# The skewing copies of the distances issued by three queues, in a two-layer decoder kernel on one core

## The chip, the cores and the metric

The kernel is one program for one core of one Trainium2 chip. The metric is the device time of one execution in microseconds (us), the median of several runs. Engines: TensorE (PE in the profile), VectorE (DVE), ScalarE (ACT), GpSimd (POOL) and SyncE (SP). A DMA is issued by an instruction in the queue of SP, ACT or POOL.

## The reference, cut to what matters

Two decoder layers over x (8 batches of 112 tokens, width 256). Each adds, in turn, a self-attention, a part that looks at the context (8 x 375 x 256), and a mixture of experts. The change lies in the context part of the first layer, a dynamic time warping (DTW) of the 375 context rows against the 112 tokens, for each batch:

```python
D = _pairwise_euclidean(small, large)         # 375 x 112
R = _dtw_cost(D)    # r = d_ij + min(up, left, diag)
i_idx, j_idx, valid = _backtrack(R, T_small, T_large)
contrib = small[i_idx] * valid[:, None].astype(small.dtype)
expanded = jnp.zeros((T_large, d), dtype=small.dtype).at[j_idx].add(contrib)
```

and `x = x + _L0_xattn_ref(ctx_1024, _layernorm(x, axis=-1))`. Everything after it (the first layer's experts, the second layer) needs its result.

## The kernel before, in words

Each engine has its own function with its instructions in the order written there; semaphores tie them together (`wait_ge`, `then_inc`). A DMA adds 16 to its semaphore when it has landed.

**Distances.** `Dd` (in `Vc_r`) holds them with the 112 tokens on partitions and, for each of B = 8 batches, S = 375 values. They are made two batches at a time (`q4` = 0 to 3): VectorE's `squares`, four activations on ScalarE (L976 to L979), and VectorE's `roots` (L1731 to L1733), whose last instruction raises `dist_ready`.

**Skewing copies.** The recurrence runs on 32 partitions, G = 4 groups of context columns (RC = 94 values each, 93 in the last, g = 3) times 8 batches; partition g * 8 + b of `Dsk` holds group g of batch b, shifted by 4 steps per group. A DMA copy for each (b, g) and for each block of token rows brings them there: its source is one run of up to 94 values in each of the block's partitions, its destination one partition. The blocks k are the rows 0 to 15, 16 to 47 and 48 to 111 (`ROW_CUTS`), with 32 copies each. Before, SyncE issues the 24 copies of g = 0 to 2 of each block (L569 for block 0, L573 for blocks 1 and 2) and GpSimd the 8 of g = 3 (L742, L745). Both take block 0 pair by pair as `dist_ready` rises.

**Recurrence.** VectorE goes through 124 columns q, each with two scans over half a group (L1768) and the minima that feed them (L1763). Before columns 1, 17 and 49 it waits for all 32 copies of block 0, 1 and 2. SyncE brings the finished cost rows to another layout behind it (L581, 56 copies), and VectorE goes on with the choices and the path (L1798 and after).

**Beside it.** Behind the squares ScalarE empties TensorE's banks of the second layer's key products (12 copies into `KcT_r`); then it waits for all three blocks of copies, because the value products are written over `Dd` (12 copies into `Vc_r`). Behind its copies GpSimd sets an edge (L746), waits for the value products and reloads the context (L751), used after the path is known.

Of the kernel before, what the change touches and what calls it, by code (L numbers as in the profile page):

```python
# [57 lines left out]
def view(t, offset, dims, parts=None):  # L58

    x = t[:] if parts is None else t[parts[0]:parts[1]]  # L60
    return bass.AP(x.tensor, x.offset + offset, [x.ap[0]] + dims)
# [8 lines left out]
def decoder_kernel(nc, A, out):  # L70
    B, T, D = A["x"].shape
# [4 lines left out]
    HB = B // 2  # L76
    HT = HB * T
    E0, F0 = A["L0_ffn_b1"].shape
    M0 = F0 // 128
    E1, _, F1 = A["L1_ffn_Wg"].shape  # L80
    NS1 = A["L1_ffn_Sg"].shape[1] // F1
    WE = KD * 2 * F1 + D
# [4 lines left out]
    G = 4  # L87
# [13 lines left out]
    with ExitStack() as ctx:  # L101
# [3 lines left out]
        def sem(name):  # L105
            return ctx.enter_context(nc.semaphore(name))
# [245 lines left out]
        act, dve, routing, scored = "act", "dve", "routing", "scored"  # L352
# [69 lines left out]
        for n in range(NG + LV):  # L422
            if n < NG and n % 2 == 0:
                r_s1[n], r_s1[n + 1] = ring.take(scored, scored)
            if LT <= n < NG + LT:
                (r_pt1[n - LT],) = ring.take(act)
            if n >= LV:
                _, _, key, first, last = value_step(n - LV)
                if first:
                    r_o1[key] = ring.open(BANKS - 2 + key[1])  # L430
                if last:
                    ring.close(r_o1[key], act)
# [44 lines left out]
        ROW_CUTS = (0, 16, 48, T)  # L477
        NBLK = len(ROW_CUTS) - 1
# [19 lines left out]
        s = {name: sem(name) for name in names}  # L498
        ctx_loaded = [sem(f"ctx_loaded{i}") for i in range(4)]
        rows_moved = [sem(f"cost_rows_moved{k}") for k in range(NBLK)]  # L500
        last_rows_moved = [sem(f"last_cost_rows_moved{k}") for k in range(NBLK)]
        cw_moved = [sem(f"segment_rows_moved{i}") for i in range(SEG)]
        xg0_loaded = [sem(f"token_rows_loaded_first{i}") for i in range(XR)]
        y0_stored = [sem(f"tile_rows_scattered{i}") for i in range(YR)]
# [18 lines left out]
        def skewed(b, g, k):  # L523

            lo, hi = ROW_CUTS[k:k + 2]
            return view(Dsk, (g * KC + lo) * RC, [[RC, hi - lo], [1, min(RC, S - g * RC)]],
                        (g * B + b, g * B + b + 1))

        def plain_rows(b, g, k):

            src = Dd[ROW_CUTS[k]:ROW_CUTS[k + 1], b, g * RC:min((g + 1) * RC, S)]
            return bass.AP(src.tensor, src.offset, [src.ap[0], [1, min(RC, S - g * RC)]])


        def step_of(seg, g):
            return 2 * seg + 1 + g

# [2 lines left out]
        def column_done(q):  # L540


            return 4 * q + (q < COLS) + min(q - 1, COLS - SH - 1) // SH
# [8 lines left out]
        def _(sp):  # L552
# [9 lines left out]
                             c_d[:, 2 * i:2 * i + 2]).then_inc(ctx_loaded[i], 16)  # L562

            sp.wait_ge(s["dsk_clear"], 1)
            for q4 in range(B // 2):
                sp.wait_ge(s["dist_ready"], q4 + 1)
                for b in (2 * q4, 2 * q4 + 1):
                    for g in range(G - 1):
                        sp.dma_start(skewed(b, g, 0), plain_rows(b, g, 0)).then_inc(rows_moved[0], 16)  # L569
            for k in range(1, NBLK):  # L570
                for b in range(B):
                    for g in range(G - 1):
                        sp.dma_start(skewed(b, g, k), plain_rows(b, g, k)).then_inc(rows_moved[k], 16)  # L573

            sp.wait_ge(s["edge_ready"], 1)
            for seg in range(SEG):
                for g in range(G):
                    n = min(RC, S - g * RC)
                    sp.wait_ge(s["dtw_op"], column_done(KC * min(step_of(seg, g) + 1, STEPS)))
                    q = seg * SC + g * KC  # L580
                    sp.dma_start(Rb[seg * B:(seg + 1) * B, :, 1 + g * RC:1 + g * RC + n],  # L581
                                 RS[g * B:(g + 1) * B, q:q + SC + 1, 1:1 + n]).then_inc(s["costs_moved"], 16)
# [63 lines left out]
            for r in range(NS1):  # L646
                f = slice(r * F1, (r + 1) * F1)
# [20 lines left out]
        def _(pool):  # L668
# [67 lines left out]
            link(nc.gpsimd.memset(RS[:, 0:KC + 1, :], BIG))  # L736

            nc.gpsimd.memset(RS[0:B, 0, 0:1], 0.0).then_inc(s["costs_clear"], 1)
            for q4 in range(B // 2):
                pool.wait_ge(s["dist_ready"], q4 + 1)  # L740
                for b in (2 * q4, 2 * q4 + 1):
                    pool.dma_start(skewed(b, G - 1, 0), plain_rows(b, G - 1, 0)).then_inc(last_rows_moved[0], 16)  # L742
            for k in range(1, NBLK):
                for b in range(B):
                    pool.dma_start(skewed(b, G - 1, k), plain_rows(b, G - 1, k)).then_inc(last_rows_moved[k], 16)  # L745
            nc.gpsimd.memset(Rb[:, :, 0:1], BIG).then_inc(s["edge_ready"], 1)  # L746

            pool.wait_ge(full, r_vc[-1].n + 1)
# [41 lines left out]
            for n in range(NT0 + LAG):  # L790
# [6 lines left out]
                if 0 <= n - (LAG + 8) < 3 * KD:  # L797
                    k, w = divmod(n - (LAG + 8), 3)
# [83 lines left out]
        def _(sc):  # L882
# [90 lines left out]
            for q4 in range(B // 2):  # L973
# [4 lines left out]
                link(nc.scalar.activation(inv[:, sl, :], inv[:, sl, :], ACT.Exp, scale=-0.5))  # L978
                nc.scalar.activation(aaB[:, sl, :], inv[:, sl, :], ACT.Square).then_inc(s["inv_ready"], 1)  # L979

            sc.wait_ge(free[act], r_bias.count)
            i = 0
            for m in range(KD):
# [2 lines left out]
                         bias=bqk[:, 1, m:m + 1])  # L986
                    i += 1
            for k in range(NBLK):
                sc.wait_ge(rows_moved[k], 16 * B * (G - 1))
                sc.wait_ge(last_rows_moved[k], 16 * B)  # L990
            for i, slot in enumerate(r_vc):
                copy(slot, Vc_r[0:CR, 2 * i * D:(2 * i + 2) * D], bank(slot)[0:CR, :])
            for n, cols in enumerate((slice(NS // 2, NS), slice(0, NS // 2))):
# [69 lines left out]
            for n in range(NG + LV):  # L1063
                if n < NG:
                    sc.wait_ge(s["heads_shifted"], n + 1)
                    if n >= NP:
                        sc.wait_ge(full, r_pt1[n - NP].n + 1)
                    for j in range(HB):
                        ins = nc.scalar.activation(  # L1069
                            Px[:, n % NP, j * T:(j + 1) * T], bank(r_s1[n])[0:T, j * T:(j + 1) * T], ACT.Exp,  # L1070
                            bias=hm[:, n % NP, 1, j:j + 1], scale=HD ** -0.5, accum_out=hm[:, n % NP, 2, j:j + 1])
                    ins.then_inc(free[scored], 1)
                if LT <= n < NG + LT:
                    m = n - LT
                    if m >= 3:
                        sc.wait_ge(s["values_used"], m - 2)
                    copy(r_pt1[m], PxT[:, m % 3], bank(r_pt1[m])[0:T, 0:HT])
                if n >= LV:
                    _, _, key, _, last = value_step(n - LV)
                    if last:  # L1080
                        copy(r_o1[key], NT[:, key[0], x_cols(key[1])], bank(r_o1[key])[:, 0:HT])
# [548 lines left out]
        def _(ve):  # L1630
# [73 lines left out]
            for i, slot in enumerate(r_pv0):  # L1704
                src = bank(slot)
                for j in range(2):
                    b = 2 * i + j
# [47 lines left out]
            def step(ins):  # L1755
                ops[0] += 1
                ins.then_inc(s["dtw_op"], 1)
                return ops[0]

            def lesser(q, part, after):  # L1760
                lo, hi = part
                ve.wait_ge(s["dtw_op"], after)
                return step(v.tensor_tensor(mtmp[:, lo:hi], RS[:, q - 1, lo:hi], RS[:, q - 1, lo + 1:hi + 1], ALU.min))  # L1763

            def scan(q, part, after):
                lo, hi = part
                ve.wait_ge(s["dtw_op"], after)
                return step(v.tensor_tensor_scan(RS[:, q, lo + 1:hi + 1], mtmp[:, lo:hi],  # L1768
                                                 Dsk[:, (q - 1) * RC + lo:(q - 1) * RC + hi],
                                                 RS[:, q, lo:lo + 1], ALU.min, ALU.add))  # L1770
# [3 lines left out]
            lu = step(v.tensor_tensor(mtmp[:, 0:RC // 2], RS[:, 0, 0:RC // 2], RS[:, 0, 1:RC // 2 + 1], ALU.min))  # L1774
            for q in range(1, COLS + 1):
                if q - 1 in ROW_CUTS[:-1]:
                    ve.wait_ge(rows_moved[ROW_CUTS.index(q - 1)], 16 * B * (G - 1))
                    ve.wait_ge(last_rows_moved[ROW_CUTS.index(q - 1)], 16 * B)
                su = scan(q, upper, lu)
                ll = lesser(q, lower, sl) if q > 1 else \  # L1780
                    step(v.tensor_tensor(mtmp[:, RC // 2:RC], RS[:, 0, RC // 2:RC], RS[:, 0, RC // 2 + 1:RC + 1], ALU.min))
                if q < COLS:
                    lu = lesser(q + 1, upper, su)
                if q % SH == 1 and SH < q <= COLS - SH:

                    lu = step(v.stream_shuffle(RS[:, q + 1:q + 1 + SH, 0], RS[:, q - SH:q, RC],
                                               [(p - B) % 32 for p in range(32)]))
                sl = scan(q, lower, max(ll, su))
                assert sl == column_done(q)
# [334 lines left out]
            for n in range(B + 2):  # L2124
# [4 lines left out]
                if n >= 2:  # L2129
                    b = n - 2  # L2130
# [97 lines left out]
```

## Time and profile before

| | |
|---|---|
| median of 3 runs | 635.02 us (634.96 to 660.84) |
| the profiled execution's own time | 631.45 us |
| its span, first to last instruction | 629.5 us |
| mean granted TensorE clock | 0.888 of full speed |
| busy: PE / DVE / ACT / POOL | 472.0 / 400.3 / 234.3 / 185.8 us |
| DMA moved | 49.07 MB, mean 78 GB/s |

The span is what the profile covers; the execution's own time has 2 us around it. Issuing a DMA isn't counted as busy. Times inside the profile are us from the first instruction.

### The profile page before, as it was taken

What the parts mean: (1) busy time and instruction counts of PE and PEld (TensorE: products, weight loads), DVE (VectorE), ACT (ScalarE), POOL (GpSimd) and SP (SyncE); (2) the same over time, 40 slices, a digit from 0 to 9 for tenths busy, and PEclk for the clock granted to TensorE, in tenths of its full rate; (3) what the DMA queues carried; (4) which work ended last, traced back from release to release, by engine and by line L of the source; (5) the groups of instructions that cost most, each with busy time, mean ns of one, the idle gap of its engine ahead of it and who ended that gap; (6) DMA issues with size and microseconds to landing.
All of it is one profiled execution on the core that took longest, in us unless ns stands there. A gap on an engine that the chain in (4) does not pass through costs nothing.

```text
span 629.5 us, 9016 instructions
## 1 busy us (share of the span) xinstructions
PE 472.0 (75%) x2802; PEld 376.3 (60%) x2802; DVE 400.3 (64%) x1352; ACT 234.3 (37%) x670; POOL 185.8 (30%) x272
## 2 busy tenths in 40 slices
PE   6988999050002288699999996899999798799980
PEld 6974547040001035598899995778777475689850
DVE  6047765999989986453543257677874155756545
ACT  2357760030000421304344303389984545034300
POOL 6003260030000002135668324511102411366354
PEclk9988999675556599869999999999999999899995
DMA  5300111139410088712212140050005401045623
GB/s 169 116 24 1 37 28 24 37 55 149 72 16 0 10 269 274 163 26 68 69 55 72 50 134 1 2 169 1 2 2 156 145 1 59 27 135 167 136 85 115
DMA packets 48801, 49.07 MB, mean 78 GB/s; under 512 B 14656, under 2 KB 41908, under 8 KB 48532
## 3 DMA queue, kind: packets, MB, share of 16 engines
q1 hardware_dynamic: 40996, 33.37, 18.8%
q0 software_dynamic: 7760, 15.14, 10.2%
q8 instruction: 23, 0.38, 0.2%
q14 instruction: 22, 0.18, 0.1%
HBM read 36.14 MB, written 9.31 MB: 72 GB/s over the span
## 4 chain that ended last, share of the span: by engine, by line
PE 51%; DVE 28%; ACT 5%; issue 4%; SPq 4%; DMA 4%; POOL 2%; another core or an unknown queue 1%; DVEq 0%; ACTq 0%; POOLq 0%
PE ps L1143 45%; DVE big L1768 7%; PE ps L1146 6%; DVE mtmp L1763 4%; SPq L573 2%; DVE big L2118 1%; DVE rk L2110 1%; DVE big L1809 1%; DVE big L1810 1%; ACT N_r L921 1%; DVE big L1843 1%; SPq L569 1%; ACT big L893 1%; DMA big<-scattered 1%; DMA big<-in_L_attn_wo 1%
## 5 line engine op out<-in xcount | busy, mean ns | idle before, releaser
L1143 PE MATMUL ps<-ident 128*128 128x128 f32 (+1 forms) x304 | 63.2, 372 | 78.9 <-DVE big L1801 60.0
L1143 PEld LDWEIGHTS ps<-ident 128*128 128x128 f32 x304 | 46.0, 233 | 86.5 <-DVE big L1801 60.4
L1143 PE MATMUL ps<-ctxT_r,big 128*128 128x128 f32 (+1 forms) x616 | 83.2, 285 | 2.5 <-issue 1.2
L1143 PEld LDWEIGHTS ps<-ctxT_r,big 128*128 128x128 f32 (+1 forms) x616 | 75.8, 191 | 7.0 <-issue 5.0
L1768 DVE TENSOR_TENSOR_SCAN big<-mtmp,big 32x47 f32<-32x47 f32 x248 | 62.6, 287 | 11.6 <-DMA big<-Vc_r 11.6
L1143 PE MATMUL ps<-big 112*128 112x112 f32 (+6 forms) x458 | 61.6, 312 | 3.7 <-issue 3.4
L893 ACT ACTIVATE big<-ps 112x448 f32<-112x448 f32 (+5 forms) x63 | 38.4, 640 | 53.6 <-PE ps L1146 34.4
L1143 PEld LDWEIGHTS ps<-big 112*128 112x128 f32 (+5 forms) x458 | 51.7, 186 | 7.9 <-issue 4.3
L893 ACT ACTIVATE ctxT_r<-ps 128x256 f32<-128x256 f32 (+3 forms) x74 | 30.9, 433 | 60.5 <-PE ps L1146 34.6
L1146 PE MATMUL ps<-ident,big 112*112 112x112 f32 (+5 forms) x289 | 40.5, 277 | 13.4 <-DVE big L2118 4.4
L1146 PEld LDWEIGHTS ps<-ident,big 112*112 112x112 f32 (+5 forms) x289 | 30.5, 144 | 27.7 <-DVE big L1843 10.2
L1069 ACT ACTIVATE big<-ps,rk 112x112 f32<-112x112 f32 x128 | 44.4, 388 | 5.8 <-DVE rk L2111 5.3
L1143 PE MATMUL ps<-big,ctxT_r 128*128 x168 | 39.6, 379 | 0.0
L700 POOL TENSOR_SCALAR veps<-mv 112x2 f32<-112x2 f32 x24 | 5.6, 233 | 110.5 <-DVE mv L1656 76.0
L1763 DVE TENSOR_TENSOR mtmp<-big 32x47 f32<-32x47 f32 x246 | 37.1, 183 | 0.0
L2053 DVE COPY big<-ps 128x256 f32<-128x256 f32 x21 | 8.9, 424 | 43.8 <-PE ps L1143 41.1
L1143 PE MATMUL ps<-N_r,ctxT_r 128*125 128x256 f32 x96 | 23.5, 409 | 16.9 <-ACT Vc_r L893 16.9
L1043 ACT ACTIVATE ctxT_r<-ps,big 128x128 f32<-128x128 f32 x84 | 24.0, 368 | 31.0 <-PE ps L1143 31.0
L866 POOL DMA_INDIRECT ctxT_r<-normed,source x29 | 29.3, 1009 | 19.3 <-issue 9.9
L1143 PEld LDWEIGHTS ps<-big,ctxT_r 128*128 128x128 f32 x168 | 30.4, 190 | 3.3
L1143 PEld LDWEIGHTS ps<-N_r,ctxT_r 128*125 128x125 f32 x96 | 19.6, 205 | 21.1 <-ACT Vc_r L893 17.4
L794 POOL DMA_INDIRECT ctxT_r<-normed,source x21 | 25.5, 1213 | 21.5 <-PE ps L1146 12.5
(269 smaller groups left out, 927.7 us busy)
## 6 DMA issues: line engine op xcount, KB each, us to landing
big<-in_L_ffn_W SPq DMA_DIRECT2D x16, 512.0 KB, 7.2
routed<-Vc_r SPq DMA_DIRECT2D x29, 128.0 KB
big<-in_ctx SPq DMA_DIRECT2D x4, 750.0 KB
ctxT_r<-in_ctx POOLq DMA_DIRECT2D x4, 750.0 KB, 20.5
big<-in_L_ffn_Wg SPq DMA_DIRECT2D x16, 128.0 KB, 2.4
big<-in_L_ffn_Wu SPq DMA_DIRECT2D x16, 128.0 KB, 2.5
big<-in_L_ffn_Wd SPq DMA_DIRECT2D x16, 128.0 KB, 2.5
normed<-N_r SPq DMA_DIRECT2D x2, 896.0 KB, 5.3
```

The lines of the kernel that those rows point to most:

```text
L569: sp.dma_start(skewed(b, g, 0), plain_rows(b, g, 0)).then_inc(rows_moved[0], 16)
L573: sp.dma_start(skewed(b, g, k), plain_rows(b, g, k)).then_inc(rows_moved[k], 16)
L794: pool.indirect_dma_start(out=Xg0[:, n % XR], out_offset=None, in_=normed0, in_offset=bass.IndirectOffsetOnAxis(ap=source[:, n:n + 1], axi ...
L866: pool.indirect_dma_start(out=Xg[:, n % XR], out_offset=None, in_=normed, in_offset=bass.IndirectOffsetOnAxis(ap=source[:, n:n + 1], axis= ...
L893: return nc.scalar.activation(dst, src, func, **kw).then_inc(free[act], 1)
L1043: ins = nc.scalar.activation(hT0[:, m % 2, j], src[:, j * 128:(j + 1) * 128], ACT.Relu, bias=b1t[:, j, m:m + 1])
L1069: ins = nc.scalar.activation(Px[:, n % NP, j * T:(j + 1) * T], bank(r_s1[n])[0:T, j * T:(j + 1) * T], ACT.Exp, bias=hm[:, n % NP, 1, j:j + ...
L1143: return nc.tensor.matmul(dst, lhsT, rhs, start=first, stop=last)
L1146: return nc.tensor.transpose(dst, src, ident[0:n, 0:n])
L1763: return step(v.tensor_tensor(mtmp[:, lo:hi], RS[:, q - 1, lo:hi], RS[:, q - 1, lo + 1:hi + 1], ALU.min))
L1768: return step(v.tensor_tensor_scan(RS[:, q, lo + 1:hi + 1], mtmp[:, lo:hi], Dsk[:, (q - 1) * RC + lo:(q - 1) * RC + hi], RS[:, q, lo:lo + ...
L2053: empty(r_y0[m], v.tensor_copy(yb0[:, m % YR], bank(r_y0[m])[:, 0:D]))
```

## The change

One function, `mover(b, g, k)`, names the queue for each copy. The last group, g = 3, stays on GpSimd in all blocks. In block 0, batches 4 and 5 go to ScalarE with their three other groups, batch 7 with g = 0 to ScalarE and with g = 1 and 2 to GpSimd. In block 1, g = 1 of batches 4 to 7 and g = 2 of batches 0 to 5 go to ScalarE, g = 2 of batches 6 and 7 to GpSimd. Everything else is SyncE's. ScalarE issues its copies after the squares and ahead of the key copies. The counts that are waited for follow the table: ScalarE's copies count on SyncE's semaphore.

```diff
+        def mover(b, g, k):
+            if g == G - 1:
+                return "pool"
+            if k == 0:
+                return {4: "act", 5: "act", 7: ("act", "pool", "pool")[g]}.get(b, "sp")
+            if k == 1:
+                return ("sp", "sp" if b < HB else "act", "act" if b < B - 2 else "pool")[g]
+            return "sp"
+
+        def moved_by(queue, k):
+            return [(b, g) for b in range(B) for g in range(G) if mover(b, g, k) == queue]
+
+        def rows_in(k):
+            n = len(moved_by("pool", k))
+            return 16 * (G * B - n), 16 * n
...
# SyncE
-            for q4 in range(B // 2):
-                sp.wait_ge(s["dist_ready"], q4 + 1)
-                for b in (2 * q4, 2 * q4 + 1):
-                    for g in range(G - 1):
-                        sp.dma_start(skewed(b, g, 0), plain_rows(b, g, 0)).then_inc(rows_moved[0], 16)
-            for k in range(1, NBLK):
-                for b in range(B):
-                    for g in range(G - 1):
-                        sp.dma_start(skewed(b, g, k), plain_rows(b, g, k)).then_inc(rows_moved[k], 16)
+            for k in range(NBLK):
+                for b, g in moved_by("sp", k):
+                    sp.wait_ge(s["dist_ready"], b // 2 + 1)
+                    sp.dma_start(skewed(b, g, k), plain_rows(b, g, k)).then_inc(rows_moved[k], 16)
...
# GpSimd, in place of its two loops of the same form
+            for k in range(NBLK):
+                for b, g in moved_by("pool", k):
+                    pool.wait_ge(s["dist_ready"], b // 2 + 1)
+                    pool.dma_start(skewed(b, g, k), plain_rows(b, g, k)).then_inc(pool_rows_moved[k], 16)
...
# ScalarE, between the squares and the key copies
+            sc.wait_ge(s["dsk_clear"], 1)
+            for k in range(2):
+                for b, g in moved_by("act", k):
+                    sc.wait_ge(s["dist_ready"], b // 2 + 1)
+                    sc.dma_start(skewed(b, g, k), plain_rows(b, g, k)).then_inc(rows_moved[k], 16)
...
# VectorE, and the same on ScalarE
-                    ve.wait_ge(rows_moved[ROW_CUTS.index(q - 1)], 16 * B * (G - 1))
-                    ve.wait_ge(last_rows_moved[ROW_CUTS.index(q - 1)], 16 * B)
+                    k = ROW_CUTS.index(q - 1)
+                    ve.wait_ge(rows_moved[k], rows_in(k)[0])
+                    ve.wait_ge(pool_rows_moved[k], rows_in(k)[1])
```

## Rows read from the trace of the kernel before

**Rows 1.** The page: shares of the chain that ended last; the scans' group.

```profile
PE 51%; DVE 28%; ACT 5%; issue 4%; SPq 4%; DMA 4%; POOL 2%; another core or an unknown queue 1%; DVEq 0%; ACTq 0%; POOLq 0%
...
L1768 DVE TENSOR_TENSOR_SCAN big<-mtmp,big 32x47 f32<-32x47 f32 x248 | 62.6, 287 | 11.6 <-DMA big<-Vc_r 11.6
```

**Rows 2.** That chain in order of time: start, us, what.

```profile
97.42 2.65 SPq L573
...
106.44 2.07 DMA big<-Vc_r
...
182.91 2.33 DMA big<-big
```

**Rows 3.** VectorE's timeline: start, us, instruction [idle before <- what ended it].

```profile
84.81 0.94 DVE L1733 SCALAR_TENSOR_TENSOR Vc_r<-Vc_r 112x750 f32<-112x750 f32 x1
...
91.06 0.30 DVE L1768 TENSOR_TENSOR_SCAN big<-mtmp,big 32x47 f32<-32x47 f32 x1 [5.20 <-DMA big<-Vc_r]
...
108.54 0.30 DVE L1768 TENSOR_TENSOR_SCAN big<-mtmp,big 32x47 f32<-32x47 f32 x1 [6.40 <-DMA big<-Vc_r]
```

**Rows 4.** The chain's SyncE issues; then landings of L569 issued 85.4 to 89.2.

```profile
86.01 0.59 SPq L569
...
89.17 0.60 SPq L569
...
DMA to landing us min/median/max: 1.8/1.9/2.3
```

**Rows 5.** L573's landings, issued 89.8-91.1, 91.1-92.3, 92.3-94.9 (x5), 107.7-116.0 (block 2).

```profile
DMA to landing us min/median/max: 2.3/2.5/4.7
...
DMA to landing us min/median/max: 4.7/7.4/7.6
...
DMA to landing us min/median/max: 6.4/7.1/7.4
...
DMA to landing us min/median/max: 2.6/2.6/2.6
```

**Rows 6.** GpSimd's landings: L742 86.0-86.5; L745 87.0-90.4 (x8), 89.9-91.9 (x5), 92.4-94.4 (x5).

```profile
DMA to landing us min/median/max: 1.6/1.6/1.6
...
DMA to landing us min/median/max: 1.9/1.9/2.1
...
DMA to landing us min/median/max: 2.0/3.8/5.9
...
DMA to landing us min/median/max: 6.8/6.9/7.1
```

**Rows 7.** Stretches: busy us (count) of PE, PEld, DVE, ACT, POOL; PEclk; DMA share; GB/s.

```profile
74.00:82.00 8.00, 8.00 (x21) 3.75 (x20) 7.57 (x11) 6.83 (x8) 1.99 (x4) 1.00 0.06 11
82.00:90.00 8.00, 8.00 (x20) 3.61 (x19) 3.20 (x5) 5.71 (x10) 4.92 (x11) 1.00 0.10 19
...
94.00:96.00 2.00, 2.00 (x9) 1.38 (x8) 2.00 (x15) 0.68 (x1) 1.04 (x3) 1.00 0.59 64
```

**Rows 8.** GpSimd's timeline.

```profile
86.04 0.96 POOL L742 DMA_DIRECT2D big<-Vc_r  x2 [2.52 <-DVE Vc_r L1733]
86.99 7.92 POOL L745 DMA_DIRECT2D big<-Vc_r  x16
```

**Rows 9.** ScalarE's timeline.

```profile
82.00 0.83 ACT L979 ACTIVATE Vc_r<-big 112x750 f32<-112x750 f32 x1
82.74 3.50 ACT L893 ACTIVATE KcT_r<-ps,bcol 128x500 f32<-128x500 f32 x6
...
124.99 4.03 ACT L893 ACTIVATE Vc_r<-ps 125x512 f32<-125x512 f32 x8 [29.40 <-DMA big<-Vc_r]
```

**Rows 10.** Who waited for whom, 66 to 215 us: total, times, longest.

```profile
PE ps L1143 <- DVE big L1801: 60.0, 1, 60.0
POOL big L754 <- DVE big L1801: 53.5, 1, 53.5
```

**Rows 11.** SyncE's timeline.

```profile
122.85 7.43 SPq L581 DMA_DIRECT2D big<-big  x10
```

More of the change, by code:

```diff
@@ L500, in decoder_kernel @@
         rows_moved = [sem(f"cost_rows_moved{k}") for k in range(NBLK)]
-        last_rows_moved = [sem(f"last_cost_rows_moved{k}") for k in range(NBLK)]
+        pool_rows_moved = [sem(f"last_cost_rows_moved{k}") for k in range(NBLK)]
         cw_moved = [sem(f"segment_rows_moved{i}") for i in range(SEG)]
@@ L738, in _ @@
             nc.gpsimd.memset(RS[0:B, 0, 0:1], 0.0).then_inc(s["costs_clear"], 1)
[L739 to L745, printed above, removed]
+            for k in range(NBLK):
+                for b, g in moved_by("pool", k):
+                    pool.wait_ge(s["dist_ready"], b // 2 + 1)
+                    pool.dma_start(skewed(b, g, k), plain_rows(b, g, k)).then_inc(pool_rows_moved[k], 16)
             nc.gpsimd.memset(Rb[:, :, 0:1], BIG).then_inc(s["edge_ready"], 1)
@@ L988, in _ @@
             for k in range(NBLK):
-                sc.wait_ge(rows_moved[k], 16 * B * (G - 1))
-                sc.wait_ge(last_rows_moved[k], 16 * B)
+                sc.wait_ge(rows_moved[k], rows_in(k)[0])
+                sc.wait_ge(pool_rows_moved[k], rows_in(k)[1])
             for i, slot in enumerate(r_vc):
```

## The prediction

> **What bounds the kernel now.** I read the page's chain of work first [rows 1]: TensorE and VectorE hold nearly all of it, but SyncE's queue stands in it with 4% of the span, all on the two lines that issue the skewing copies. In time order [rows 2] that chain goes through the issue of the copies to one copy's landing at 108.5, and from there through the recurrence to 182.9. So in this stretch the end is set by when the copied rows arrive. The VectorE timeline [rows 3] prices it: the distances end at 84.81 + 0.94 = 85.75, the recurrence then sits 5.20 us until block 0 (16 rows) is complete at 91.06, and 6.40 us at column 17 (102.14 to 108.54) until block 1 (32 rows) is. These 11.6 us are all that the 248 scans of the recurrence wait for, in the whole run [rows 1]; block 2 is on time. Sixteen columns took 102.14 - 91.06 = 11.1, or 0.69 us each, and the 108 columns from 108.54 to 182.9 the same 0.69: it runs at VectorE's own pace otherwise. Thus the change can win at most 11.6 us (1.8%) here.
>
> Why the rows are late: SyncE issues a copy every (89.17 - 86.01) / 5 = 0.63 us [rows 4], of either size, and 24 of them per block; each lands 1.8 to 2.6 us after its issue when nothing disturbs it [rows 4, 5]. The 16 DMA engines are 6 to 10% busy between 74 and 90 us [rows 7]. It is the issuing, not the moving, that takes the time. One disturbance is in the trace: SyncE's copies issued from 91.7 on land up to 7.6 us later, those of block 2 again 2.6 [rows 5]; one issue at 97.42 took 2.65 us [rows 2]. GpSimd's eight copies of block 2, issued from 86.99 + 8 x 0.49 = 90.9 on, land 3.8 to 7.1 us after issue, while its block 1 copies, issued before, took 1.9 to 2.1 [rows 6, 8]. The DMA share is 0.59 from 94 to 96 [rows 7]. GpSimd's 64-row copies, one per 0.50 us and all into neighbouring partitions, seem to hold up everybody's landings from about 92 to 99.5.
>
> **The change, part by part.** By the mover table block 0 has 15 copies on SyncE, 7 on ScalarE, 10 on GpSimd (24, 0, 8 before); block 1 has 12, 10, 10; block 2 is as before (24, 0, 8).
>
> Block 0. The last pair of batches is free at 85.75; SyncE issued its six last copies from 86.01 to 89.17 and the last landed 1.9 later, at 91.06 [rows 3, 4]. Now SyncE has three for that pair: 86.01, 86.64, 87.27 (steps of 0.63), landing 87.27 + 1.9 = 89.2. GpSimd started that pair at 86.04 [rows 8] and has four copies in place of two: the last issue at 86.04 + 3 x 0.49 = 87.5, landing 1.6 later [rows 6] = 89.1. ScalarE can issue only once its last square (82.00 + 0.83) is done [rows 9], six copies of batches 4 and 5 and one of batch 7. No row shows a DMA issue on ScalarE. Bounds: GpSimd's 0.49 as the low end, SyncE's stalled 2.65 as the high end. I take SyncE's 0.63, as it is the same kind of copy and the same kind of queue: seventh issue at 82.83 + 6 x 0.63 = 86.6, landed at 88.5. It stays behind the others' 89.2 up to 0.74 us an issue. Block 0 is complete at 89.2: gain 91.06 - 89.2 = 1.9 us. Column 17 is then reached at 102.14 - 1.9 = 100.3.
>
> Block 1. SyncE's twelve run from 87.9 to 94.9 (11 x 0.633), ScalarE's ten from 87.3 to 93.0, GpSimd's ten from 88.0 to 92.4. With undisturbed landings (2.1 to 2.5, [rows 2, 5]) the last is in at 97.2, before it is needed at 100.3, and the whole 6.40 is gone. But GpSimd's block 2 copies follow its ten: they begin at 92.9, 2.0 later than now. If the disturbance moves with them, whatever SyncE issues from 91.7 + 2.0 = 93.7 on lands late, and that is its last two copies of block 1 (94.2 and 94.9). The one like the last was issued at 92.9 before and landed about 7.2 later (the second of the five issued from 92.3, whose longest is 7.4 and median 7.1, [rows 5]), at 100.1; moved by 2.0 it is 102.1. So 102.1 - 100.3 = 1.8 of the 6.4 stays, and the gain is 4.6. I take this value, since the same eight copies are issued at the same pace by the same queue with the same neighbours.
>
> Block 2. SyncE's 24 now start at 95.5; 23 x 0.633 with one stall of 2.65 - 0.59 gives the last issue at 112.1 and, 2.6 later [rows 5], 114.8. Column 49 is reached at 102.1 + 32 x 0.69 = 124.2: 9.4 us of cover. If it were lacking, each further us would be paid in full.
>
> What is moved past. ScalarE's twelve key copies stood right behind its squares, at 82.74 [rows 9]; they are now queued behind 17 issues, 17 x 0.63 = 10.8 us, so TensorE's key products stall once its banks are full. I cost this at nothing: ScalarE then waits 29.40 us for the moved rows before it may write the values [rows 9], and behind the values TensorE waits 60.0 us for the recurrence and what follows it, GpSimd 53.5 [rows 10]. Without that cover the 10.8 would be paid. That wait now ends with block 2 at about 115 in place of 124.99, so values and the reload of the context come some 10 us sooner, not later. On GpSimd the memset behind the copies (86.99 + 7.92 = 94.91, [rows 8]) comes 2.0 later, at 96.9; the first who asks for it is SyncE at about 113. The added waits for the distances ride on the copies: the copy at 86.01, which carried one, took the same 0.59 [rows 4]. SyncE's copies of the cost rows began at 122.85 [rows 11] and can begin 10 us sooner; the last still waits for the last column. Behind the recurrence every step is released by it, and the weight loads are too, so the gain passes on whole.
>
> A rule speaks against the change. The Trainium skill, page "DMA: Bandwidth & Descriptors", section "Issuing engines are not separate DMA queues", says that DMAs from all engines run on the same 16 engines and that issuing from several saves only the sequencer's time, usually small beside the transfer. By it the gain would be near nothing, 635.0, which is rival (e).
>
> Here the rows say that the issuing is the larger part: 24 issues of 0.63, 15.2 us, stand against a last landing of 1.9.
>
> **The sum.** 1.9 + 4.6 = 6.5 us. Profiled execution: 631.45 - 6.5 = 624.9, its span 629.5 - 6.5 = 623.0. The median of the runs, 635.02, lies 3.6 above the profiled one; on it the forecast is 628.5.
>
> **Rivals.**
> (a) The disturbance misses block 1, or is not what it seems: no wait at column 17, 1.9 + 6.4 = 8.3, or 626.7. For it: only two copies are caught, by about 1 us. Against: SyncE's block 2 copies (twice the rows) now join the same moment.
> (b) The disturbance doesn't hang on block 2 but on VectorE beginning the recurrence, which in the rows is at 91.06, just when the landings turn late. Then it begins at 89.2 and meets eight of GpSimd's block 1 copies. GpSimd's first late landings are 1.55 apart (90.9 + 3.8 = 94.7, and 91.9 + 5.9 = 97.8 two copies on, [rows 6]), the first 3.6 after the recurrence began. Eight of them from 89.2 + 3.6 = 92.8 on end at 92.8 + 7 x 1.55 = 103.7 (they are half as large, so this is its upper end); the wait at column 17 is 3.4 and the gain 1.9 + 3.0 = 4.9: 630.1. SyncE's copies being late too speaks against it. The Trainium skill, page "SBUF — State Buffer", section "SBUF: two separate sides", has such a lock: some VectorE instructions keep GpSimd from writing descriptors. It calls copies issued from SyncE immune, which these rows don't bear out if this is the cause.
> (c) SyncE's and ScalarE's copies share what makes their descriptors, so both queues together go at 0.63. From 86.0 two of ScalarE's and three of SyncE's are left: last issue 88.5, landed 90.4, gain 0.7. Then 22 from 89.2, last at 102.5, with the stall 104.6, landed 106.7: total gain 1.9, or 633.1. No row has both queues at work, for or against.
> (d) Slower: ScalarE issues much slower than SyncE. Its 17th copy starts at 82.83 + 16p and lands 2.1 later; from p = 1.48 us on this is after 108.54, and all beyond is loss. At p = 2.0 it is 116.9, 8.4 slower, 643.4; to pass 2% it takes 2.3. Against it: every SyncE issue but one is at 0.59.
> (e) The change does not do what it says: the 16 engines, not the queue, set the pace of the copies, so that three queues only interleave and each block is complete when it was, 635.0. Against it: their share of 6 to 10% while SyncE issued without a pause [rows 7]. For it: the share of 0.59 once two queues carried large copies.
>
> **How the numbers follow.** Forecast 0.45; (a) 0.20; (b) 0.13; (c) 0.10; (d) 0.05; (e) 0.07. The range takes in the forecast, (a), (b) and, at its end, (c): 626.0 (a, with an early landing or so) to 633.2, about 0.85 with what can lie between. 2% is 12.7 us, about what a measurement of this kernel can tell from no change. More than that is beyond the 11.6 that can be had here; I leave 0.03 for it. Slower by over 2% needs p above 2.3: 0.02. Within 2%: 0.95.
>
> **What would show it.** Right: the first scan at about 89.2; an idle of 1 to 3 us on VectorE at column 17, or none (a); no idle at column 49; the last scan at about 176.1; ScalarE's issues near 0.6 us; GpSimd's first late landing moved to about 93. Step by step wrong: ScalarE issues above 0.74 delay block 0; SyncE issues stretched between 86 and 95 mean (c); late landings already from 89 mean (b). The forecast is wrong as a whole if the recurrence itself runs slower than 0.69 a column beside three queues, or if a stretch behind 183 grows by what this one has lost.

## The result and the profile after

The first comparison gave a ratio of the changed kernel to the one before of 0.9843, 95% interval 0.981 to 0.9875: on 635.02 us that is 625.1 (623.0 to 627.1), against a forecast of 628.5. The profiled execution took 624.15 us, its span is 622.2 us (629.5 before). I timed the same kernel three more times: 0.9923 (0.9879 to 0.9967), 0.9889 (0.9851 to 0.9926) and 0.9908 (0.987 to 0.9947). The mean of the four is 0.989, a gain of 6.9 us. The first comparison left out every execution more than 1.5% above the fastest of its own kernel, and so set aside three of the changed kernel (631.4, 633.9 and 634.2 us, granted clock 0.873 to 0.876) while executions of the kernel before up to 637.6 us counted; with those three in, the ratio of the means is 0.989.

VectorE's timeline of the kernel after, for [rows 3]: the last instruction of the distances, the only two waits for rows, and the last scan.

```profile
84.30 0.94 DVE L1749 SCALAR_TENSOR_TENSOR Vc_r<-Vc_r 112x750 f32<-112x750 f32 x1
...
88.85 0.30 DVE L1784 TENSOR_TENSOR_SCAN big<-mtmp,big 32x47 f32<-32x47 f32 x1 [3.51 <-DMA big<-Vc_r]
...
102.25 0.30 DVE L1784 TENSOR_TENSOR_SCAN big<-mtmp,big 32x47 f32<-32x47 f32 x1 [2.32 <-DMA big<-Vc_r]
...
176.28 0.30 DVE L1784 TENSOR_TENSOR_SCAN big<-mtmp,big 32x47 f32<-32x47 f32 x1
```

The last scan of the kernel before:

```profile
182.58 0.30 DVE L1768 TENSOR_TENSOR_SCAN big<-mtmp,big 32x47 f32<-32x47 f32 x1
```

The distances end at 84.30 + 0.94 = 85.24, half a us sooner than before, so all else is counted from there. The first scan comes 3.6 us behind them (5.3 before), the idle at column 17 is 2.32 in place of 6.40, and no other is left. The last scan ends at 176.58, 91.3 us behind the distances (182.88 and 97.1 before). That is a gain of 5.8 us: 1.7 at block 0, 4.1 at block 1. The spans differ by 7.3 us: 0.5 ahead of the distances' end, these 5.8, and 1.0 behind the last scan.

Who holds block 1? The chain in order of time, for [rows 2], names the last of SyncE's copies (start, us, what):

```profile
94.35 7.87 DMA big<-Vc_r
```

And the landings of GpSimd's copies (issued 91.8 to 95.8, block 2 but for one) and of SyncE's (91.1 to 94.3) answer to [rows 5, 6]:

```profile
L755 POOL DMA_DIRECT2D big<-Vc_r x9: 496/506/514, 91.8 to 95.8; - x9
...
DMA to landing us min/median/max: 3.0/7.2/7.9
...
L586 SPq DMA_DIRECT2D big<-Vc_r x6: 588/596/604, 91.1 to 94.3; - x6
...
DMA to landing us min/median/max: 2.4/6.4/7.9
```

SyncE's twelfth copy of block 1 is issued at 94.35 and lands 7.87 us later, at 102.2. It is not alone: the five of the twelve that are issued from 91.8 on take 3.0, 5.9, 6.9, 7.8 and 7.9 us, the ones before them 2.2 to 2.4. ScalarE's queue, for which there was no row, has this one (all 17 copies):

```profile
L995 ACTq DMA_DIRECT2D big<-Vc_r x17: 597/601/609, 81.8 to 92.1; - x17
```

(92.1 - 81.8) / 16 = 0.64 us a copy. SyncE's issues beside it take 0.59 to 0.63 us but for one of 0.76 at 85.81; from there to 94.35 it has one copy in 0.66 us, against 0.63 before. What stood behind the copies on ScalarE moved as feared, and cost nothing; its timeline, for [rows 9], and TensorE's:

```profile
92.83 5.22 ACT L903 ACTIVATE KcT_r<-ps,bcol 128x500 f32<-128x500 f32 x9 [10.51 <-issue]
...
113.45 4.16 ACT L903 ACTIVATE Vc_r<-ps 125x512 f32<-125x512 f32 x8 [9.57 <-DMA big<-Vc_r]
...
93.56 9.61 PE L1159 MATMUL ps<-ctxT_r,N_r 128*128 128x500 f32 x16 [5.89 <-ACT KcT_r L903]
```

TensorE stood 5.89 us, ScalarE's key copies came 10 us late, and still 9.57 us of ScalarE's old wait of 29.40 are left. TensorE's granted clock was 1.00 up to that stop and 0.51 (the lower of its two levels, 1.2 of 2.4 GHz) from 93.5 to 99, then 1.00 again; the 9.57 us cover that too.

### The profile page after: what moved, and what is told of

The parts are those of the page before. It is cut to its first block, busy times and chain, and to the rows that moved or that the text cites. A ratio compares the mean times of both kernels' runs of the same rounds, so it can differ in the third digit from the quotient of the medians.

```text
span 622.2 us, 9017 instructions
## 1 busy us (share of the span) xinstructions
PE 473.4 (76%) x2802; PEld 376.1 (60%) x2802; DVE 400.5 (64%) x1352; ACT 234.1 (38%) x670; POOL 188.1 (30%) x276
## 4 chain that ended last, share of the span: by engine, by line
PE 53%; DVE 28%; ACT 6%; DMA 4%; issue 4%; POOL 2%; SPq 1%; another core or an unknown queue 1%; DVEq 0%; ACTq 0%; POOLq 0%
PE ps L1159 46%; DVE big L1784 7%; PE ps L1162 6%; DVE mtmp L1779 4%; DVE big L2135 1%; DVE rk L2127 1%; SPq L586 1%; DMA big<-Vc_r 1%; DVE big L1826 1%; DVE big L1827 1%; ACT N_r L931 1%; DVE big L1860 1%; ACT big L903 1%; DMA ctxT_r<-normed,source 1%; DMA big<-in_L_attn_wo 1%
## 5 line engine op out<-in xcount | busy, mean ns | idle before, releaser
L1011 ACT ACTIVATE big<-big,ones 112x1500 f32<-112x1500 f32 x2 | 3.1, 1537 | 81.7 <-DVE big L1834 81.7
L931 ACT ACTIVATE N_r<-X,shift,rstd 112x256 f32<-112x256 f32 x32 | 17.4, 592 | 36.9 <-POOL shift L720 36.9
```

Of the source, the lines that this page charges most:

```text
L931: nc.scalar.activation(N[:, b, :], X[:, b, :], ACT.Identity, bias=shift[:, b:b + 1], scale=rstd[:, b:b + 1]).then_inc(s["norm_ready"], 1)
```

## The experiments

Idles and distances below are VectorE's, read as above; "behind the distances" counts from the end of the last instruction that makes them.

**The changed kernel again** (three times).

> The changed kernel once more, unchanged, to see how far its runs spread and how the granted clock of each goes with its time. Theory 1 (the profile of the change is the whole effect): the gain is that of the waits, 1.7 us at block 0 and 4.1 at block 1, so runs at a clock of 0.88 to 0.89 lie 6 to 7 us under the kernel before's. Theory 2 (something more is gained, outside this stretch): they lie about 10 us under it. Either way an idle of 2 to 3 us at column 17.

> The changed kernel a third time, for its spread. If the gain is that of the waits and 0.7 us on the path, 6.5 us, the ratio of its fast runs to those of the kernel before is 0.990, within 0.985 to 0.994. If the first ratio, 0.984, was right, it is 0.984 again.

> The changed kernel a fourth time, beside its two mended versions. Ratio to the kernel before about 0.989, the mean of the three so far.

The ratios stand above. In the three profiles the last scan ends 91.9, 92.2 and 91.5 us behind the distances, with 2.3 to 3.1 us of idle at column 17 in all four: the stretch of the change repeats within 0.8 us. What differs lies behind it: stretches from the path to the end, in the profile of the changed kernel (first fence) and of its fourth measurement (second); busy us of PE, PEld, DVE, ACT, POOL, then the granted clock:

```profile
465.00:542.00 77.00, 66.46 (x345) 48.84 (x343) 37.78 (x125) 30.03 (x71) 19.77 (x37) 0.98 0.26 77
```

```profile
465.00:542.00 77.00, 67.60 (x310) 46.91 (x310) 35.71 (x121) 31.16 (x76) 16.75 (x34) 0.88 0.25 74
```

The same 77 us hold 345 matmuls at a clock of 0.98 and 310 at 0.88. From the last scan to the end of the span it took 445.6 us in the one and 454.7 in the other; in the kernel before 446.6. The mean granted clock of the two executions is 0.889 and 0.875: up to 9 us more or less go with the clock that an execution happens to be granted.

The times and clocks of all executions settle how much is left without it. Through those of the kernel before and of the changed kernel that took under 645 us and whose clock is on record (42 and 32 of them), one line for each kernel with a common slope gives 4.2 us for every 0.01 of mean granted clock, and at equal clock 5.5 us (4.9 to 6.1) between the kernels. Theory 1 holds: the change itself gives the 5.0 to 5.8 us that four profiles show (the expected 6 to 7 was a little high), and the first ratio is the outlier of four.

**GpSimd's block 2 copies held back.**

```diff
             for k in range(NBLK):
+                if k == 2:
+                    pool.wait_ge(s["dtw_op"], column_done(18))
                 for b, g in moved_by("pool", k):
```

> GpSimd issues its eight copies of block 2 only when column 18 of the recurrence is done. Theory A (these copies hold up everybody's landings): SyncE's last copy of block 1 lands about 2 us after its issue in place of 7.9, the idle at column 17 (2.32 us) is gone, the last scan ends 2.3 us sooner than with the change, and 2.3 us come off the time. GpSimd's eight copies still land late, up to 7 us, and SyncE's block 2 copies beside them, but nobody waits. Theory B (VectorE's recurrence holds up GpSimd's copies and these the rest): GpSimd's ten copies of block 1 still run beside the scans from 89 on, so an idle of 1 us or more stays.

Ratio 0.9832 (0.9767 to 0.9897). SyncE's copies issued from 91.1 to 94.4 land after 2.1 to 2.6 us. One idle is left on VectorE:

```profile
89.47 0.30 DVE L1786 TENSOR_TENSOR_SCAN big<-mtmp,big 32x47 f32<-32x47 f32 x1 [3.50 <-DMA big<-Vc_r]
```

The last scan ends 89.0 us behind the distances, 2.4 sooner than with the change, as theory A had it. The late landings are not gone; they went along to where the eight copies now are (SyncE's issued beside them take up to 8.2 us):

```profile
L757 POOL DMA_DIRECT2D big<-Vc_r x8: 503/506/521, 102.2 to 105.7; - x8
...
DMA to landing us min/median/max: 3.2/7.0/8.0
```

**The recurrence held back instead.**

```diff
+            ve.wait_ge(rows_moved[1], rows_in(1)[0])
+            ve.wait_ge(pool_rows_moved[1], rows_in(1)[1])
             lu = step(v.tensor_tensor(mtmp[:, 0:RC // 2], RS[:, 0, 0:RC // 2], ...
```

> VectorE waits for block 1 before column 1, so that no scan runs while the copies of blocks 0 and 1 and GpSimd's of block 2 are issued. Theory A: the late landings stay as they are, the last copy of block 1 lands at about 102 and the first scan starts there, 13 us later than with the change. Theory B: with VectorE idle all copies land about 2 us after issue, the last of block 1 at about 96.5, and the first scan starts there.

VectorE's timeline and the landings of SyncE's copies issued 92.6 to 93.9:

```profile
102.00 0.20 DVE L1792 TENSOR_TENSOR mtmp<-big 32x47 f32<-32x47 f32 x1 [17.26 <-DMA big<-Vc_r]
...
DMA to landing us min/median/max: 7.7/7.8/8.0
```

Not one scan ran between 85 and 102, and the copies were as late as ever. So rival (b), and with it the lock of VectorE against GpSimd, falls: theory A again. The first scan starts at 102.35, as theory A had it. The single execution took 636.06.

**Two queues.** ScalarE's 17 copies back on SyncE.

```diff
-                return {4: "act", 5: "act", 7: ("act", "pool", "pool")[g]}.get(b, "sp")
+                return {7: ("sp", "pool", "pool")[g]}.get(b, "sp")
             if k == 1:
-                return ("sp", "sp" if b < HB else "act", "act" if b < B - 2 else "pool")[g]
+                return ("sp", "sp", "sp" if b < B - 2 else "pool")[g]
```

> ScalarE's 17 copies go back to SyncE; GpSimd keeps its ten, ten and eight. SyncE has 22 copies in blocks 0 and 1. Main theory (each queue's issue time is what counts): block 0 complete at about 89.8 (first scan 1 us later than with three queues), SyncE's last copy of block 1 issued near 103.5 with one stalled issue, an idle of about 4 to 5 us at column 17, last scan 3 to 4 us later than with three queues; about 3 us faster than before. Rival (ScalarE's queue adds nothing, the copies only interleave): the same column times as with three queues. ScalarE's key copies start at 82.7 again and TensorE does not fall to half clock between 90 and 99: if that clock matters to the whole, the runs' clocks are less spread than with three queues.

```profile
89.14 0.30 DVE L1784 TENSOR_TENSOR_SCAN big<-mtmp,big 32x47 f32<-32x47 f32 x1 [4.17 <-DMA big<-Vc_r]
...
104.45 0.30 DVE L1784 TENSOR_TENSOR_SCAN big<-mtmp,big 32x47 f32<-32x47 f32 x1 [4.22 <-DMA big<-Vc_r]
```

The last scan is 93.9 us behind the distances: 3.2 of the 5.8 us come from GpSimd's extra copies, 2.6 from ScalarE's queue (3 to 4 were expected). Ratio 0.996 (0.9925 to 0.9995), 2.5 us; at equal clock, by the line above with all kernels in it, 2.6 (1.7 to 3.5). The rival, that ScalarE's queue adds nothing, falls. The clocks of its executions (0.873 to 0.888) spread as those of the changed kernel do (0.872 to 0.887 in the fourth measurement), though here TensorE's clock stays at 1.00 from 85 to 103; so nothing points to TensorE's stop at 88 to 94 as what spreads them.

**The same copies in another order.** Neighbours in time are no longer neighbours in partition.

```diff
-            return [(b, g) for b in range(B) for g in range(G) if mover(b, g, k) == queue]
+            turn = (0, 4, 1, 5, 2, 6, 3, 7) if queue == "pool" and k == 2 else range(B)
+            return [(b, g) for b in turn for g in range(G) if mover(b, g, k) == queue]
```

> GpSimd's eight copies of block 2 go to the batches 0, 4, 1, 5, 2, 6, 3, 7 in place of 0 to 7, so that two consecutive copies never have destinations within the same four partitions (24 to 27, 28 to 31). Theory A1 (copies crowd because four in a row share one way into the memory): their landings come closer together, the last of block 1 lands 2 us or more sooner than with the change, and the idle at column 17 falls from 2.3 to 2.8 to under 1 us. Theory A2 (it is the mere volume and pace of GpSimd's copies, wherever they go): the idle stays between 2 and 3 us.

> The changed kernel with GpSimd's block 2 copies in the order 0, 4, 1, 5, 2, 6, 3, 7, now timed. In its first profile the idle at column 17 was gone, so 2.3 to 2.8 us under the changed kernel: a ratio to the kernel before of about 0.985.

In the first profile, GpSimd's nine copies issued from 92.9 to 96.9 and SyncE's from 91.6 to 96.7:

```profile
L756 POOL DMA_DIRECT2D big<-Vc_r x9: 496/506/514, 92.9 to 96.9; - x9
...
DMA to landing us min/median/max: 2.7/3.9/4.4
...
L587 SPq DMA_DIRECT2D big<-Vc_r x9: 588/592/607, 91.6 to 96.7; - x9
...
DMA to landing us min/median/max: 2.3/3.6/5.0
```

The same eight copies, sizes, queue and pace, and the longest landing is 4.4 in place of 7.9 (SyncE's 5.0). The idle at column 17 is gone, the last scan 89.0 us behind the distances. In the profile of the timed run the order did less: the eight took up to 5.8 us and SyncE's up to 6.1, 0.70 us of idle stayed, and the last scan is 89.7 us behind the distances. Both idles are under 1 us, as theory A1 had it, so the order of the destinations matters. But in neither profile are the late landings gone (a 64-row copy of SyncE that nothing disturbs takes 2.6 us), so theory A2, volume and pace, keeps a part. And the new order also never has two neighbouring partitions in a row: that the fours are what counts, and not mere nearness, is not tested.

The packets tell the same. GpSimd's 64-row copies move in packets of 1488 B, four rows each, 16 to a copy; SyncE's in packets of 376 B, one row each. In order, the 1488-B packets of the changed kernel took 163 ns on average and up to 1206; in the new order 81 and 185 (88 and 538 in the timed run's profile). SyncE's took up to 782 ns beside the first and up to 164 (432) beside the second.

The ratio is 0.9884 (0.9837 to 0.9931), which the clock's spread does not tell from the changed kernel's 0.9908 beside it.

**And in the kernel before**, the same order, and, separately, the copies held back (the waiting lines of block2_held, put into its loop).

```diff
             for k in range(1, NBLK):
-                for b in range(B):
+                for b in ((0, 4, 1, 5, 2, 6, 3, 7) if k == 2 else range(B)):
                     pool.dma_start(skewed(b, G - 1, k), plain_rows(b, G - 1, k)).then_inc(last_rows_moved[k], 16)
```

> The kernel before with only this order changed. If four neighbouring partitions in a row are the cause of the late landings, SyncE's train of block 1 has no issue of 2.65 us and the idle at column 17 falls from 6.40 to about 4.3 us, as it did when these copies were held back. If the cause is GpSimd's volume, or anything tied to three queues, it stays at 6.4.

> The kernel before, with GpSimd's eight copies of block 2 issued when column 18 is done. Theory A: SyncE's train of block 1 copies runs without the issue of 2.65 us, the last is issued at 104.4 and lands at 106.5; the idle at column 17 falls from 6.4 to about 4.4 us and 2.0 us come off the time. So the change's gain at column 17 (4.1) plus what is left there (2.3) minus this 2.0 is what the issuing alone costs.

```profile
105.59 0.30 DVE L1768 TENSOR_TENSOR_SCAN big<-mtmp,big 32x47 f32<-32x47 f32 x1 [4.31 <-DMA big<-Vc_r]
```

4.31 us with the new order and 4.28 with the copies held back, in place of 6.40 [rows 3]: either edit alone takes the 2.1 us off the old kernel that the crowding cost it, as expected, and what is left is issue time. Their profiled executions took 630.13 and 629.09; neither has enough of them for a ratio.

Where do the 2.1 us come from? The issue of 2.65 us at 97.42 [rows 2] is gone in both. In the kernel before it ran beside one 8-KB packet of the queue that brings instructions, from 97.25, which took 2.43 us; in these two runs that packet took 0.31 and 0.47 us, and no SyncE issue took over 0.7. The changed kernel has such a pair as well (1.53 us from 95.29, and an issue of 1.60 at 95.61). So SyncE most likely stood for its next instructions, which came late through the same crowd; no run separates this.

**Block 2 on SyncE alone.** `mover` sends g = 3 to GpSimd only for k below 2.

> GpSimd has no copy of block 2; SyncE issues all 32, g = 0 to 3 in turn, so that only every fourth goes to the partitions 24 to 31. Theory A: no late landings anywhere, no idle at column 17, last scan 2.3 us sooner than with the change; SyncE's 32nd copy is issued at 114.6 and lands at 117.3, before column 49 is reached at 122. ScalarE begins the value copies at 117 in place of 113, at no cost. Rival: 64-row copies into these partitions are slow whoever issues them; then landings of 4 us and more stand among SyncE's, but none before block 1 is complete.

> All 32 copies of block 2 on SyncE, a second time beside the changed kernel. By the profiles 2.3 us under the changed kernel, so a ratio to the kernel before of about 0.985 if the first 0.9816 was helped by the granted clock.

SyncE's copies issued from 94.7 to 115.1, block 2 but for one:

```profile
L586 SPq DMA_DIRECT2D big<-Vc_r x33: 588/591/600, 94.7 to 115.1; - x33
...
DMA to landing us min/median/max: 2.5/2.6/2.7
```

The same 64-row copies into the same partitions 24 to 31, but 2.5 us apart with three others between, and in packets of one row, land in 2.6 us. Which of the three cures them (pace, what lies between, or the packets) this run doesn't tell. No idle at column 17 in either profile, last scan 89.0 us behind the distances in both. ScalarE begins the value copies at 117.8, at no cost. Ratios 0.9816 (0.9758 to 0.9873) and 0.989 (0.9841 to 0.9939). By the profiles this version and the one held back are level, 2.4 us under the change and 8.2 under the kernel before, with the new order 0 to 0.7 behind them. The times show little of it. Beside the changed kernel (0.989 to 0.9908) the clock's spread hides the difference, and the expected 0.985 was missed here as with the new order, though it lies inside both intervals. At equal clock the three lie 7.3 (held back), 6.3 (new order) and 5.4 us (all on SyncE) under the kernel before, each to about 1 us, against the change's 5.5: only the one held back is clear of the change.

## Why the prediction was right or wrong

**The range failed.** Its lower end, 626.0, was the best case of the waits, 8.3 us, and nothing else. The first ratio lies at 625.1, below it: 9.9 us of gain, where the waits gave 5.8. The step at fault is the one that takes the bounds of the waits for the range of the time. It put at nothing how far two sets of executions of one program differ through the clock that they are granted, although the three runs shown and the profiled execution, 3.6 us apart, hinted at it. Measured in its place: four comparisons of the same two kernels give 0.9843 to 0.9923, 5 us from end to end; 0.01 of mean clock goes with 4.2 us; and the three executions set aside in the first comparison are worth about 3 us of its ratio. The mechanism in the first comparison's profile is the one that I described. That the mean of four, 628.1, and the forecast, 628.5, nearly meet is in part luck: at equal clock the gain is 5.5, not 6.5.

**Block 0: right.** 1.9 forecast, 1.7 measured; ScalarE's price, for which there was no row, was taken as 0.63 and is 0.64.

**Block 1: right in mechanism and close in size.** The disturbance did move with GpSimd's block 2 copies and did catch SyncE's last two, but not only these: its last five, from 91.8 on, landed late. I had read its start in the kernel before as 91.7, though [rows 5] has a landing of 4.7 us already for the copy issued at 91.1. I had the last landing at 102.1 and it was at 102.2, which is in part luck: the distances ended 0.5 us sooner, so that behind them it came 17.0 us in place of 16.4. The idle was 2.32 in place of 1.8, since the recurrence did begin sooner and the landing didn't follow, and the gain 4.1 us in place of 4.6. What held SyncE's issue for 2.65 us was left open and only carried along as a stall.

**The rest of the path: 0.7 us more than forecast.** From the last scan to the first step of the path (TensorE's product in between) it took 41.0 us in place of 41.7. "The gain passes on whole" was not exact; but 40.9 to 42.1 us stand in the other profiles, those of kernels alike in this stretch too, so I don't put it down to the change. It is VectorE's wait for that product, 1.26 us before and 0.57 after; the sum had no term for it, and it is 0.44 to 1.58 in the others.

**Covers: right.** No idle at column 49, ScalarE's late key copies free, the wait that hides them down to 9.57 us.

**Rivals.** (a) falls by the idle at column 17, although holding the copies back gives 8.2 of its 8.3 us. (b) falls by the recurrence held back. (c) falls: while both ran, ScalarE's issues took 0.60 us and SyncE's 0.59 to 0.63, one of 0.76 apart; together they went at 0.32 to 0.33 us a copy, not at 0.63. (d) ScalarE's 0.64 is far from 1.48. (e) falls by two_queues, where the queue taken away costs its share, and by the stretch from 88 to 91 of the changed kernel: three queues moved 62 GB/s there with undisturbed landings (1.9 to 2.4 us), about as much as the kernel before from 94 to 96 (64 GB/s), when landings were late. So the rule of the Trainium skill, page "DMA: Bandwidth & Descriptors", section "Issuing engines are not separate DMA queues", holds in its first half (another queue saves only issue time) and not in its "usually small": here the issue time taken off was 5.8 us of waiting. Of the 6.40 us at column 17 in the kernel before, 4.3 were issue time and 2.1 the crowding.

## What to carry to other kernels

Many small copies from one queue go at the queue's issue pace, 0.6 us each here; count issues, not bytes, then deal them out, and look at what stands behind them on the queue that takes them. After dealing them out, look at which destination partitions follow each other: here eight 64-row copies in a row into eight neighbouring partitions delayed every queue's landings. Another order costs nothing and took off part of it; moving them to where nobody waits, or among other copies, took off all of the waiting. And before giving a range of 1% for a kernel with changing TensorE clock, ask how far the same program's own executions lie apart.

## What the runs showed that I had not expected

That the order of eight copies matters so much. Each moves 64 x 372 bytes = 23.8 KB. In the kernel before the four into partitions 24 to 27 land 1.6 us apart, 15 GB/s, while copies of SyncE into other partitions, issued meanwhile, take up to 7.6 us as well (8.1 in the changed kernel). The four behind them, into 28 to 31, then land 0.3 to 0.5 us apart, so the 1.6 is the rate of a crowd at its start and not of every such copy. In alternation with 28 to 31 none of the eight takes over 4.4 us in one profile and over 5.8 in the other.

The Trainium skill, page "SBUF — State Buffer", section "Door 1: The DMA port swizzle", puts four neighbouring partitions on one port. The runs fit this, as an order that changes between the fours helps. They don't show the rate: the 8 partitions' port would take 27 GB/s by an estimate from that page (435 over 16), and the landings lie below it at first and above it afterwards.

That others' copies are held up as well, the page "DMA: Bandwidth & Descriptors" of the Trainium skill, section "Back-pressure in remote DMA", says of copies between cores: stalled writes stall the other queues of the same engine. What is seen here within one core fits it; that the stall sits in the shared engines is not shown.

Why GpSimd's 32-row copies, 12 KB each at the same pace, do no harm at 24 GB/s stays open. They differ from the larger ones in their packets too, 744 B in place of 1488.
